# Second attention: where TensorE multiplies the probabilities by the values within a turn

## The reference

```
c = tanh(mixed_q @ wfq + bfq + (mean(mixed_q) @ wfg + bfg))      # split into heads
P = sigmoid(sum(c * up)) * key_len;   Z = sigmoid(sum(c * uz)) * key_len
G = -(j - P[..., None]) ** 2 * 2.0 / Z[..., None] ** 2           # j: the key's position
scores = einsum('bhqd,bhkd->bhqk', q, k) / sqrt(D) + G
probs = softmax(scores, axis=-1)
ctx = einsum('bhqk,bhkd->bhqd', probs, v)
```

## Time and profile before

| | us |
|---|---|
| median of 3 runs | 2055.53 |
| lowest and highest | 2054.86, 2056.92 |
| the profiled execution's own time | 2056.59 |
| its span, first to last instruction | 2054.9 |
| PE busy over the span | 1708.0 (83%) |
| DVE busy | 1286.1 (63%) |
| ACT busy | 938.8 (46%) |
| stage of the second attention with turns | about 1292 to 1994 of the span |

### The profile page before, as it was taken

The page is one execution under the profiler, slowest core; times in us unless marked ns, Lnnn a source line. Parts: engine busy times, 40 slices in busy tenths (PEclk is TensorE's granted clock), DMA queues, the critical chain, the costliest instruction groups (busy, mean ns, idle before and its releaser), DMA issues. The chain is left out here.

```text
span 2054.9 us, 27643 instructions
## 1 busy us (share of the span) xinstructions
PE 1708.0 (83%) x11088; PEld 559.9 (27%) x11088; DVE 1286.1 (63%) x1810; ACT 938.8 (46%) x1087; POOL 596.3 (29%) x313
## 2 busy tenths in 40 slices
PE   5889999999999999985998504788888888888873
PEld 3233333333333333323444200111111111111111
DVE  3555555555655565615101777888888888888816
ACT  2324444444444444341221300576777777777770
POOL 1347676767575757680000300000000000000000
PEclk8989999999999999996999755899999999999996
DMA  3000000000000000001000245011100120111000
GB/s 62 1 2 1 2 1 1 2 1 1 1 1 1 2 1 1 2 1 57 0 0 0 49 152 88 2 40 21 36 21 20 21 55 22 21 21 21 2 3 23
DMA packets 47713, 39.03 MB, mean 19 GB/s; under 512 B 19518, under 2 KB 42594, under 8 KB 47586
## 3 DMA queue, kind: packets, MB, share of 16 engines
q1 hardware_dynamic: 41394, 35.71, 7.6%
q10 hardware_dynamic: 6192, 1.57, 0.5%
HBM read 25.53 MB, written 10.49 MB: 18 GB/s over the span
## 5 line engine op out<-in xcount | busy, mean ns | idle before, releaser
L1229 ACT ACTIVATE probs<-ps_e 128x1024 f32<-128x1024 f32 x512 | 498.1, 1022 | 253.6 <-PE ps_e L1290 253.6
L353 POOL TENSOR_TENSOR acc<-acc,probs 128x1024 f32<-128x1024 f32 (+3 forms) x256 | 502.2, 1962 | 164.6 <-ACT probs L383 150.0
L383 ACT ACTIVATE probs<-ps_e 128x1024 f32<-128x1024 f32 (+1 forms) x320 | 288.7, 902 | 424.7 <-PE ps_e L529 275.3
L1350 DVE TENSOR_REDUCE maxpart<-ps_x 128x2 f32<-128x1024 f32 x351 | 427.9, 1219 | 66.1 <-PE ps_x L1254 63.5
L607 DVE TENSOR_REDUCE maxpart<-ps_x 128x2 f32<-128x1024 f32 (+2 forms) x320 | 339.4, 1061 | 207.5 <-PE ps_x L453 120.9
L544 PE MATMUL ps_o<-probs,v 128*64 128x512 f32 (+3 forms) x1280 | 307.4, 559 | 1.7 <-ACT pv_raw L390 0.9
L1300 PE MATMUL ps_o<-probs,v 128*9 128x512 f32 x2048 | 267.5, 595 | 46.2 <-ACT probs L1229 30.4
L1254 PE MATMUL ps_x<-krows,qrows 60*128 60x512 bf16 x702 | 151.6, 400 | 143.9 <-DMA qrows<-g_rows 71.6
L1354 DVE TENSOR_REDUCE maxpart<-ps_y 128x1 f32<-128x512 f32 x322 | 220.2, 684 | 17.8 <-PE ps_y L1254 14.8
L1290 PE MATMUL ps_e<-qrows,krows 62*128 62x512 bf16 x1024 | 218.8, 381 | 8.3 <-ACT probs L1229 4.3
L1254 PE MATMUL ps_y<-krows,qrows 60*128 60x512 bf16 x322 | 128.6, 399 | 8.1 <-DVE maxpart L1354 0.2
(11 more groups left out here) (222 smaller groups left out, 1536.0 us busy)
## 6 DMA issues: line engine op xcount, KB each, us to landing
qrows<-q_rows SPq DMA_DIRECT2D x64, 192.0 KB
k_rows<-parts_k SPq DMA_DIRECT2D x6, 512.0 KB
q_rows<-parts_q SPq DMA_DIRECT2D x6, 512.0 KB
krows<-k_rows SPq DMA_DIRECT2D x8, 384.0 KB, 7.3
qrows<-g_rows SPq DMA_DIRECT2D x64, 48.0 KB
mrow<-maxrow SPq DMA_DIRECT2D x128, 2.0 KB
raw_h<-in_L_ffn_h_w SPq DMA_DIRECT2D x2, 1024.0 KB, 6.8
g_rows<-parts_a SPq DMA_DIRECT2D x6, 256.0 KB
```

Source lines behind the costliest of these rows:

```text
L353: pool.tensor_tensor(acc[:, u % 2, :, o:], acc[:, u % 2, :, o:], probs[:, turn % RING, :, o:], ALU.add)\
L383: act.activation(probs[:, turn % RING, :, o:], ps_e[:, turn % 2, :, o:], ACT.Exp, scale=1.0 / math.sqrt(D0))\
L1229: act.activation(probs[:, HG * (turn % 2) + hh], ps_e[:, e % 2], ACT.Exp).then_inc(s_ex, 1)
L1350: dve.reduce_max(maxpart[:, at:at + op[2]], ps_x[:, 0:op[2], :], AX.X).then_inc(s_xf, 1)
```

## The change

Only the order of work on TensorE within a turn changes. Both value products of the turn before now stand together, behind the scores of the second head and two operations of the plan. The operation that used to follow the product of head 0 is issued ahead of the pair. No instruction is added or removed.

```diff
@@ the loop over the heads of a turn, TensorE @@
                     for op in rest[:1]:
                         ring(op)
                     rest = rest[1:]
-                    if hh % 2 == 0 and turn > 0:
-                        pv(turn - 1, hh // 2)
-                        if len(rest) > HG - 1 - hh:
-                            ring(rest[0])
-                            rest = rest[1:]
+                    if hh == 1:
+                        for op in rest[:1]:
+                            ring(op)
+                        rest = rest[1:]
+                        if turn > 0:
+                            for j in range(2):
+                                pv(turn - 1, j)
                 for op in rest:
                     ring(op)
```

## The result

The changed kernel takes 2146.75 us (median of 4 runs, 2145.42 to 2147.69), the kernel before 2056.23 us beside it. The ratio is 1.0439, with a 95% interval of 1.0421 to 1.0457. That is 90.5 us more, where 65 us were forecast; the range ended at 2132 us. The direction and most of the size came as predicted. The rest came from a cause that the prediction had named as a rival, with 5 in 100.

A forecast was written before the change was run, and what follows sets the result against it. VectorE, fed late by TensorE, was taken to bound the kernel. Turns with maxima add 63.4 us, turns without 2.3 us, the start takes 0.7 us back: 65 us, median 2120.5 us, range 2109 to 2132 us.

The forecast's parts named there:

- What bounds the stage: VectorE is the fullest engine, busy 14.38 of 16.17 us in three turns, and the maxima wait for TensorE's order.
- The pair's price: On TensorE, two value products together cost 1.84 us from start to next start, instead of 1.96 us.
- The gap: VectorE idles 1.21 us each turn before the maxima while TensorE runs the pair and the third head's scores.
- the unit of 48.55 us: Length of one unit in the new order, walked through all engines; the old order gives 44.27 us.
- the turns without maxima: Turns 119 to 127 at the stage's end: 4.58 us each instead of 4.32 us, 2.3 us over 9 turns.
- The sum: Whole run: 63.4 us from turns with maxima plus 2.3 us, less 0.7 us at the start, make 65 us.
- Much slower: TensorE's clock falls: Rival: TensorE's clock drops to 1.2 GHz, the pair takes 1.84 us more; ten such turns make 2141 us; 5 in 100.
- TensorE's busy share of 75%: TensorE in the new unit is busy 36.62 of 48.5 us, down from 83%; 76% elsewhere had clock 1.00.
- the prediction's own walk: All engines followed step by step through one unit with the trace's prices: 44.27 us old order, 48.55 us new.
- The price of a low stretch: At the lower clock, VectorE's gap behind a pair was to grow by some 2.1 us a turn.
- ten such turns: Ten turns with the pair at the lower clock level would bring the run to 2141 us.
- The faster one: Rival: TensorE is what counts, its waits, entries and drains come off, 1983 us; with the 2029 us case, 3 in 100.

The follow-up runs named there:

- fill_placed: Changed kernel with score matmuls of heads 0 and 1 issued twice, three times in a unit's last and first turn; 2122.54 us.
- pair_no_op: Changed kernel with one of the two operations ahead of the pair of products moved to just behind the pair; 2122.03 us.
- The fills: Changed kernel with score matmuls of heads 0 and 1 repeated: twice 2129.73 us, three times 2137.29 us, three times in two turns of eight only 2122.54 us.

## Why the prediction was right in direction and short in size

- **What bounds the stage** held: the time followed VectorE's idle time before the maxima (+92.7 us for +90.5 us), not TensorE's waits before the products (-44.2 us), nor those before products and scores together (-1.9 us).
- **The pair's price**, 1.84 us from start to start, was the row's in the pair shown at a clock of 1.00.
- **The gap** of 1.21 us a turn, and the unit of 48.55 us (48.47 measured), held. So did the turns without maxima. On TensorE after the change, the scores of two turns that follow each other:

```profile
2064.10 0.60 PE L1290 MATMUL ps_e<-qrows,krows 62*128 62x512 bf16 x4
...
2068.68 0.60 PE L1290 MATMUL ps_e<-qrows,krows 62*128 62x512 bf16 x4
```

  4.58 us, as forecast, where it was 4.32 us.
- **The sum** of 65 us is what fill_placed, with its clock at 1.00, measures as 66.3 us.
- **The step that failed** is the rival "Much slower: TensorE's clock falls", in its chance and in its place in the sum. The prediction argued that TensorE's busy share of 75% would be safe, since the turns without maxima show 76% at a clock of 1.00. The step from a mean busy share to a clock of 1.00 is what failed. In the undisturbed unit of the changed kernel TensorE is busy for 77% (37.52 of 48.47 us), about as the prediction had it, and yet the clock fell 16 times in the stage. pair_no_op, with 82% over its stage (slowed matmuls count in it), had 18 long pairs, and the kernel before, with 83%, none. By its own list, in which the forecast is wrong "if the clock falls", the prediction failed here.
- **What makes the clock fall stays open.** The fills show that more work on TensorE takes the low stretches away. The new order bunches the work, with idle time of TensorE between the bunches, and the prediction's own walk had this; but no run shows that the bunching is what counts. How busy TensorE was in the 4.4 us before does not tell a fall from none. Here are the kernel before, once in each unit, with a wait of 1.05 us in it and a clock that stays up, and then pair_no_op just ahead of a pair of 3.47 us:

```profile
1340.80:1345.20 4.40, 2.68 (x22) 0.67 (x25) 3.37 (x5) 3.54 (x5) 0.00 (x0) 1.00 0.12 21
1342.01 1.04 PE L1300 MATMUL ps_o<-probs,v 128*9 128x512 f32 x8 [1.05 <-ACT pv_raw L1235]
...
1524.91:1529.31 4.40, 3.30 (x23) 0.74 (x15) 3.33 (x8) 3.04 (x4) 0.00 (x0) 1.00 0.00 0
```

  TensorE was busy for 61% in the first and for 75% in the second.
- **The price of a low stretch** was set too high for one (about 2.1 us of gap; the pair shown took 1.69 us more), and "ten such turns" were offered as a bad case, outside the range. There were 16, and the 25 us come to 1.6 us each.

The page TensorE: Matmul & The Clock Gate of the Trainium skill describes this kind of loss (section A second HAM failure mode: psum-queue depth-cycling): short idle times between groups of matmuls make the clock swing between its two levels. The trace agrees, with a granted clock of 0.97 over the stage and units of 48.5 to 51.6 us. The kernel before, which has short idle times too, shows no such swing.

- **The rivals on the other side** fell. The faster one needed TensorE to be what the rest waits for; the wait before the products went (46.2 us became 2.0 us), but it came back before the scores (8.3 us became 50.6 us), and VectorE's next operation was late by more. A gain does arrive when the products stay apart.

## What to carry to other kernels

Where one engine feeds another through single buffers, place foreign work by the longest time that it keeps the feeder away, not by its sum: one product of 0.98 us between two feeds cost next to nothing, two of them 1.2 us of the other engine's time in each turn. When a reordering makes gaps on TensorE, do not take a mean busy share for a promise about the clock: 83% and 76% were at 1.00 here, 82% and 78% were not. Read the granted clock afterwards, and count in beforehand that the group that is waited for may run at half of it. To tell the two losses apart, give TensorE harmless matmuls in its gaps: what then goes away was the clock's, less what the added matmuls cost themselves.

## What the runs showed of the hardware

Repeating score matmuls, 4 more in each turn and 8 more in two of eight, changes no result and made the kernel 24 us faster at best (2146.75 to 2122.54 us), by keeping the granted clock at 1.00 instead of 0.97. A clock that is 3% lower on average cost about as much as if TensorE had set the pace all the time, since the low stretches fell on the pairs: 1.7 us of 48.5 us in a unit is 3.5% of the stage. VectorE, which does set the pace, was waiting for just these pairs. And two groups of 4 products side by side cost 1.84 us, not twice 0.98 us; that saving of 0.12 us is real, and small beside the 1.21 us gap that the pair opens on VectorE.
